# Norm offsets and relu moved to GpSimd, a causal mask in 64-row halves, and new instruction orders in the attention stage of an adaLN transformer block

## What is computed

```
mod = (silu(c) @ wmod) -> sa, ca, ga, sb, cb, gb          # one row of 256 each per sequence
h = layernorm(x) * (1 + ca) + sa
q, k, v = split(h @ w_qkv); rope(q), rope(k)               # 16 heads of 16
q, k = elu(q * scale) + 1, elu(k * scale) + 1              # the features
out_t = (q_t . sum_{s<=t} k_s v_s) / (q_t . sum_{s<=t} k_s)  # causal linear attention
x = x + ga * (out @ w_out)
h = layernorm(x) * (1 + cb) + sb
x = x + gb * moe(h)                                        # top 2 of 8 experts, gelu, 256 -> 1024 -> 256
```

## Time and profile before

| what | value |
|---|---|
| time, median of 3 runs | 820.7 us (819.55 to 820.79) |
| the profiled execution's own time | 825.53 us |
| its span | 823.2 us |
| busy: TensorE, VectorE, ScalarE, GpSimd | 737.3, 663.8, 580.3, 514.3 us |
| attention stage, about | 0 to 378 us |
| routing | 378 to 411 us |
| expert stage, about | 411 to 820 us |

### The profile page before, as it was taken

How to read it: one execution, slowest core, us unless ns; L and a number is a source line. 1 busy time by engine, 2 the same in 40 slices (tenths; PEclk the granted TensorE clock), 3 DMA queues, 4 the chain that set the end, 5 groups by cost and what they waited for, 6 DMA issues and landing times.

```text
span 823.2 us, 26404 instructions
## 1 busy us (share of the span) xinstructions
PE 737.3 (90%) x7949; PEld 540.3 (66%) x7949; DVE 663.8 (81%) x1488; ACT 580.3 (71%) x1103; POOL 514.3 (62%) x504
## 2 busy tenths in 40 slices
PE   6599999999999999973489999999999999999994
PEld 3366666666666666652367777777777777777772
DVE  2789999999999999965857777778777877777773
ACT  1478888888888888862057777777677767677762
POOL 3547576766666575744746666666676667667653
PEclk9799999999999999995589999999999999999998
DMA  6214333333333333310023333343334334343320
GB/s 207 86 41 126 107 115 111 107 108 105 111 113 114 109 116 115 112 53 32 21 79 75 73 71 69 68 78 70 73 73 76 66 69 78 66 76 70 74 31 0
DMA packets 52814, 68.78 MB, mean 84 GB/s; under 512 B 8864, under 2 KB 44080, under 8 KB 52736
## 3 DMA queue, kind: packets, MB, share of 16 engines
q0 software_dynamic: 18176, 27.06, 17.5%
q1 hardware_dynamic: 34560, 40.61, 16.0%
HBM read 46.50 MB, written 22.05 MB: 83 GB/s over the span
## 4 chain that ended last, share of the span: by engine, by line
PE 59%; DVE 16%; issue 10%; ACT 8%; POOL 3%; DMA 1%; DVEq 1%; another core or an unknown queue 0%; ACTq 0%; SPq 0%; POOLq 0%
PE hidden L1334 15%; PE bank L1350 15%; PE hidden L1336 8%; PE bank L1352 7%; PE bank L1189 5%; PE hidden L1172 3%; DVE amlo L511 2%; DVE nb L452 2%; PE bank L1172 2%; ACT feat L969 2%; ACT rb L968 2%; DVE rb L498 2%; DVE hT L475 2%; DVE st L432 2%; ACT qstT L932 1%
## 5 line engine op out<-in xcount | busy, mean ns | idle before, releaser
L1334 PE MATMUL hidden<-qstT,w1hi_k 128*128 128x256 f16 x1136 | 200.2, 274 | 1.1 <-DVE am L723 1.1
L1336 PE MATMUL hidden<-qstT,w1lo_k 128*128 128x128 f16 x1136 | 195.5, 220 | 0.0
L1350 PE MATMUL bank<-w,amhi 128*128 x568 | 188.6, 379 | 0.4
L1352 PE MATMUL bank<-w,amlo 128*128 x568 | 154.8, 273 | 0.0
L729 DVE TENSOR_TENSOR amlo<-am,amhi 128x512 f16<-128x512 f32 x142 | 98.4, 693 | 62.6 <-ACT am L1064 50.8
L919 POOL DMA_INDIRECT out_dram<-x,si x71 | 121.9, 1717 | 36.5 <-issue 27.4
L1334 PEld LDWEIGHTS hidden<-qstT,w1hi_k 128*128 x1136 | 111.7, 98 | 14.9 <-issue 1.3
L1336 PEld LDWEIGHTS hidden<-qstT,w1lo_k 128*128 x1136 | 111.7, 98 | 1.1
L1189 PE MATMUL bank<-wq,hT 128*128 128x256 f32 (+1 forms) x256 | 102.9, 528 | 9.2 <-DVE hT L475 9.1
L1063 ACT ACTIVATE amhi<-am 128x512 f16<-128x512 f32 x142 | 88.5, 623 | 12.6 <-DVE am L723 7.6
L1350 PEld LDWEIGHTS bank<-w,amhi 128*128 128x128 f16 x568 | 55.5, 98 | 62.3 <-issue 2.6
(11 more groups left out here) (203 smaller groups left out, 1814.2 us busy)
## 6 DMA issues: line engine op xcount, KB each, us to landing
stage<-in_L_ffn_w_dram SPq DMA_DIRECT2D x32, 512.0 KB, 4.1
xt<-in_L_attn_x_dram SPq DMA_DIRECT2D x32, 128.0 KB, 2.1
out_dram<-x SPq DMA_DIRECT2D x32, 128.0 KB, 1.7
ffn_rows<-h SPq DMA_DIRECT2D x32, 128.0 KB, 3.3
ffn_rows<-am SPq DMA_DIRECT2D x32, 128.0 KB, 3.1
am<-mod_rows SPq DMA_DIRECT2D x16, 128.0 KB, 3.6
mod_b<-mod_rows SPq DMA_DIRECT2D x8, 256.0 KB, 3.6
w<-in_L_wmod_dram SPq DMA_DIRECT2D x6, 256.0 KB, 4.4
```

The costliest lines, as they stand in the source:

```text
L1334: t.matmul(dst.rearrange("p (q n) -> p q n", q=2), w1s[0][k][g][:, w_], both, start=(k == 0), stop=False)
L1336: last = t.matmul(dst[:, P:2 * P], w1s[1][k][g][:, w_], both[:, 0, :], start=False, stop=(k == KT - 1))
L1350: t.matmul(y[:, :], ghi[:, m.p, c_m], w2s[mt // 2][:, bass.ds(w_, 2 * D)], start=(mt == 0), stop=False)
L1352: last = t.matmul(y[:, D:2 * D], glo[:, m.p, c_m], w2s[mt // 2][:, bass.ds(w_, D)], start=False, stop=(mt == MT - 1))
```

## The change

- The norm offset `nb` is no longer one VectorE instruction. VectorE writes minus the mean (`nm`, a 128x2 tensor_scalar, in an order slot after `ve`), and GpSimd multiplies it with rstd (`nb`, after `rs`).
- The relu of the features is no longer on ScalarE. GpSimd does it as a new step `rl` (128x512, f32, maximum with 0), and `f` waits for it too.
- The mask is added by four matmuls of 64 rows and 256 columns for a group in place of two of 128 rows and 512 columns. Key row 0 of a half is never masked by the triangle, so that it is used to mask all late keys for early queries. GpSimd fills 22 constants instead of 12 for this.
- All five orders are new.

```diff
-ORDER_PE = (("aT", 4), ("ear", 3), ("pj", 4), ("sc1", 3), ("hT", 0), ("pv0", 3), ("Tk", 2), ("h2T", 6), ("v", 0),
-            ("Tq", 2), ("lg", 6), ("pv1", 3), ("state", 2), ("sc0", 2), ("qk", 0))
-ORDER_DVE = (("f", 2), ("st", 0), ("st2", 5), ("mv", 0), ("mv2", 5), ("ve", 0), ("sl0", 3), ("nb", 0), ("rope", 1),
-             ("x1", 4), ("stl", 3), ("hTe", 0), ("sl1", 3), ("wlo", 1), ("den", 3), ("rec", 3), ("vlo", 0), ("at", 3))
-ORDER_POOL = (("shk", 2), ("rs", 0), ("slo", 2), ("R", 1), ("xm2", 5), ("h2", 5), ("wb", 2))
-ORDER_ACT = (("exp", 2), ("sh0", 3), ("shq", 2), ("sth", 3), ("aTe", 4), ("whi", 1), ("xn", 0), ("xn2", 5),
-             ("sh1", 3), ("kTs", 2), ("h2Te", 6), ("vhi", 0), ("qTs", 2), ("lge", 6))
-ORDER_SP = (("ldx", 0), ("ld", 1), ("ro", 6), ("modgb", 6), ("gb", 6), ("modg", 6), ("modb", 7), ("so", 4))
+ORDER_PE = (("aT", 4), ("ear", 3), ("sc1", 3), ("pv0", 3), ("pj", 4), ("Tk", 2), ("state", 2), ("h2T", 6), ("hT", 0),
+            ("pv1", 3), ("Tq", 2), ("v", 0), ("lg", 6), ("sc0", 2), ("qk", 0))
+ORDER_DVE = (("f", 2), ("st2", 5), ("sl0", 3), ("st", 0), ("mv2", 5), ("mv", 0), ("stl", 3), ("ve", 0), ("nm", 0),
+             ("rope", 1), ("sl1", 3), ("x1", 4), ("hTe", 0), ("den", 3), ("wlo", 1), ("rec", 3), ("vlo", 0),
+             ("at", 3))
+ORDER_POOL = (("shk", 2), ("slo", 2), ("rs", 0), ("nb", 0), ("R", 1), ("xm2", 5), ("wb", 2), ("rl", 1), ("h2", 5))
+ORDER_ACT = (("exp", 2), ("sh0", 3), ("shq", 2), ("sth", 3), ("whi", 1), ("aTe", 4), ("sh1", 3), ("xn", 0),
+             ("kTs", 2), ("xn2", 5), ("h2Te", 6), ("qTs", 2), ("vhi", 0), ("lge", 6))
+ORDER_SP = (("ldx", 0), ("ro", 6), ("modg", 6), ("modb", 7), ("so", 5), ("ld", 0), ("modgb", 6), ("gb", 6))
...
-            def offset(m):
-
-                wait(dve, a_["rs"], m.n + 1)
-                wait(dve, a_["xn"], m.n, NC)
-                wait(dve, a_["xn2"], m.n - NORM2)
-                v.scalar_tensor_tensor(out=nb[:, :], in0=mv[:, :, 0], scalar=-1.0, in1=rstd[:, :],
-                                       op0=ALU.mult, op1=ALU.mult).then_inc(a_["nb"], 1)
+            def negated(m):
+
+                wait(dve, a_["mv"], m.n + 1, NC)
+                wait(dve, a_["mv2"], m.n - NORM2 + 1)
+                wait(dve, a_["nb"], m.n)
+                v.tensor_scalar(neg_mean[:, :], mv[:, :, 0], -1.0, None, ALU.mult).then_inc(a_["nm"], 1)
...
             def features(m):
 
                 wait(dve, a_["exp"], m.n + 1)
+                wait(dve, a_["rl"], m.n + 1)
...
+            def offset(m):
+
+                wait(pool, a_["rs"], m.n + 1)
+                wait(pool, a_["nm"], m.n + 1)
+                carry(pool)
+                g.tensor_tensor(nb[:, :], neg_mean[:, :], rstd[:, :], ALU.mult).then_inc(a_["nb"], 1)
...
+            def positive(m):
+
+                wait(pool, a_["R"], m.n + 1)
+                carry(pool)
+                g.tensor_scalar(rb[:, :], ra[:, :], 0.0, None, ALU.max).then_inc(a_["rl"], 1)
...
-            def relu_exp(m):
+            def exponent(m):
                 wait(act, a_["R"], m.n + 1)
                 wait(act, a_["slo"], m.n)
-                v.activation(rb[:, :], ra[:, :], ACT.Relu)
                 v.activation(feat[:, :], ra[:, :], ACT.Exp).then_inc(a_["exp"], 1)
...
-                for odd in range(2):
-                    t.matmul(bank[5 + odd].rearrange("p (h t) -> p h t", t=P), ident_b[:, :],
-                             later[:, :].rearrange("p (u t) -> p u t", u=1).broadcast_to([P, 4, P]),
-                             start=True, stop=False, skip_group_check=True)
+                half = P // 2
+                for late_q in range(2):
+                    for odd in range(2):
+                        r = slice(odd * half, (odd + 1) * half)
+                        t.matmul(bank[5 + odd].rearrange("p (h t) -> p h t", t=P)[:, :, late_q * half:(late_q + 1) * half],
+                                 mask_row[r, late_q, :],
+                                 later[r, late_q, :].rearrange("p (u t) -> p u t", u=1).broadcast_to([half, 4, half]),
+                                 start=(late_q == 0), stop=False, skip_group_check=True)
```

More of the change, by code:

```diff
@@ L58 @@
 Q_SCALE = WS * float(HD ** -0.25)
-ORDER_PE = (("aT", 4), ("ear", 3), ("pj", 4), ("sc1", 3), ("hT", 0), ("pv0", 3), ("Tk", 2), ("h2T", 6), ("v", 0),
-            ("Tq", 2), ("lg", 6), ("pv1", 3), ("state", 2), ("sc0", 2), ("qk", 0))
-ORDER_DVE = (("f", 2), ("st", 0), ("st2", 5), ("mv", 0), ("mv2", 5), ("ve", 0), ("sl0", 3), ("nb", 0), ("rope", 1),
-             ("x1", 4), ("stl", 3), ("hTe", 0), ("sl1", 3), ("wlo", 1), ("den", 3), ("rec", 3), ("vlo", 0), ("at", 3))
-ORDER_POOL = (("shk", 2), ("rs", 0), ("slo", 2), ("R", 1), ("xm2", 5), ("h2", 5), ("wb", 2))
-ORDER_ACT = (("exp", 2), ("sh0", 3), ("shq", 2), ("sth", 3), ("aTe", 4), ("whi", 1), ("xn", 0), ("xn2", 5),
-             ("sh1", 3), ("kTs", 2), ("h2Te", 6), ("vhi", 0), ("qTs", 2), ("lge", 6))
-ORDER_SP = (("ldx", 0), ("ld", 1), ("ro", 6), ("modgb", 6), ("gb", 6), ("modg", 6), ("modb", 7), ("so", 4))
+ORDER_PE = (("aT", 4), ("ear", 3), ("sc1", 3), ("pv0", 3), ("pj", 4), ("Tk", 2), ("state", 2), ("h2T", 6), ("hT", 0),
[7 more added lines that the diff above has]
+ORDER_SP = (("ldx", 0), ("ro", 6), ("modg", 6), ("modb", 7), ("so", 5), ("ld", 0), ("modgb", 6), ("gb", 6))
 NORM2 = 5
-BOTH_NORMS = ("ve", "rs", "nb")
+BOTH_NORMS = ("ve", "nm", "rs", "nb")
 LAG_C = 2
@@ L136, in adaln_block @@
         ident16 = sb("ident16", [P, P], F16)
-        ident_b = sb("ident_b", [P, P], BF16)
-        later = sb("later", [P, P], BF16)
+        mask_row = sb("mask_row", [P, 2, P], BF16)
+        later = sb("later", [P, 2, P // 2], BF16)
         upto = sb("upto", [P, P], F16)
@@ L161, in adaln_block @@
         nb = sb("nb", [P, 2])
+        neg_mean = sb("neg_mean", [P, 2])
         h = sb("h", [P, D])
@@ L266, in counters @@
             return {k: sem(prefix + k) for k in names.split()}
-        a_ = counters("a_", "st mv ve rs nb xn hT hTe v vhi vlo qk rope R exp f shq shk slo Tq qTs Tk kTs"
+        a_ = counters("a_", "st mv ve nm rs nb xn hT hTe v vhi vlo qk rope R rl exp f shq shk slo Tq qTs Tk kTs"
                             " state sth stl ear sc0 sh0 sl0 sc1 sh1 sl1 pv0 pv1 den rec at aT aTe pj"
@@ L384, in carry @@
             eng.sem_inc(s_carry, 1)
-        POOL_CONST = 16
-        POOL_TWO, POOL_EROW = 37, 50
+        POOL_CONST = 26
+        POOL_TWO, POOL_EROW = 47, 60
         POOL_IDENT, POOL_FIRST = 2, 4
@@ L563, in _ @@
                 "st": first_stats, "mv": lambda m: mean_var(m, 0, "st", "mv"),
-                "ve": steadied, "nb": offset, "hTe": h_modulated, "vlo": v_low,
+                "ve": steadied, "nm": negated, "hTe": h_modulated, "vlo": v_low,
                 "rope": rope, "f": features, "sl0": lambda m: scores_low(m, 0), "sl1": lambda m: scores_low(m, 1),
@@ L753, in attention_constants @@
                 link(g.memset(ident16[:, :], 0.0))
-                link(g.memset(ident_b[:, :], 0.0))
-                link(g.memset(later[:, :], 0.0))
+                link(g.memset(mask_row[:, :, :], 0.0))
+                link(g.memset(later[:, :, :], 0.0))
                 link(g.memset(v16[:, :, 0, :, HD:VW], 1.0))
@@ L758, in attention_constants @@
                 link(g.memset(state[:, :, :, :], 0.0))
[L759 to L763, removed]
+                diagonal(ident16)
+                link(g.affine_select(out=upto[:, :], in_=upto[:, :], compare_op=ALU.is_ge, fill=0.0, base=0,
+                                     pattern=[[1, P]], channel_multiplier=-1))
+                half = P // 2
+                for u in range(2):
+                    r = slice(u * half, (u + 1) * half)
+                    for late_q in range(2):
+                        link(g.affine_select(out=mask_row[r, late_q, :], in_=mask_row[r, late_q, :],
+                                             compare_op=ALU.not_equal, fill=1.0, base=-half * late_q,
+                                             pattern=[[1, P]], channel_multiplier=-1))
+                    link(g.affine_select(out=later[r, :, :], in_=later[r, :, :], compare_op=ALU.is_ge, fill=MASKED,
+                                         base=0, pattern=[[0, 2], [1, half]], channel_multiplier=-1))
+                    link(g.memset(mask_row[u * half:u * half + 1, 0, 0:half], 0.0))
+                    link(g.memset(mask_row[u * half:u * half + 1, 0, half:P], 1.0))
+                    link(g.memset(later[u * half:u * half + 1, 0, :], MASKED))
                 assert link.n == POOL_CONST, link.n
@@ L785, in root @@
                 wait(pool, a_["ve"], m.n + 1)
-                wait(pool, a_["nb"], m.n)
                 wait(pool, a_["xn"], m.n, NC)
@@ L836, in rotated @@
                 g.tensor_tensor(ra[:, :], ra[:, :], rb[:, :], ALU.add).then_inc(a_["R"], 1)
+            def positive(m):
+                wait(pool, a_["R"], m.n + 1)
+                carry(pool)
```

(7 more changed lines are left out.)

## The result

| what | before | after |
|---|---|---|
| time, median | 820.7 us | 854.4 us (852.74 to 855.23, 4 runs) |
| ratio to before, 95% interval | | 1.0402 [1.0377, 1.0427] |
| the profiled execution's own time, its span | 825.53, 823.2 us | 854.35, 852.6 us |

The change makes the kernel 4.0% slower. The forecast was slower too, but by 7 us; measured are 33.7 by the medians, and 854 lies above the range of 800 to 842. The profiled execution of before was 4.8 above its median and that of after is at its median, so the two traces differ by 28.8 only.

What follows compares the result with a forecast made beforehand. VectorE was taken to bound the attention stage, 10.50 us an iteration; 30 x (10.35 - 10.50) = -4.5, 7 x 1.6 = +11.2, start +1 and drain -1 made +6.7, so 832 profiled and 828 as median; range 800 to 842.

Steps and rivals of the forecast that it cites:

- as walked: VectorE and GpSimd: `xm2` runs between the halves of `wlo`, which run 7.1 to 7.7 and 8.4 to 9.0.
- the 0.32 and 0.18 taken: GpSimd: `nb` taken to run 0.32, near a 128x32 product, with 0.18 ahead of it waiting for `rs`.
- I take 0.7, near the cast: GpSimd: duration taken for `rl`, near the 0.61 cast of 128x512, the only one-input row of that length.
- from above 1.27: GpSimd: upper bound for `rl`, from the two-input sum of 128x512.
- my own walk: Attention stage: one new iteration laid out from the start of `f`, 10.35 ordinarily and 11.95 with `wb`.
- `ve` "unblocked": VectorE: only instructions with two SBUF inputs were said to exclude GpSimd's; `ve` and `nm` end at 3.6, after `stl` at 3.4.
- TensorE and its clock: TensorE: full clock, 3 us idle in 40, not the bound; mask saving of 0 to 0.6 an iteration counted as nothing.
- `wb` at 1.6: GpSimd: `wb` between `xm2` and `rl` once in four iterations, 1.6 more each, seven times, +11.2.
- Rival B: GpSimd: `rl` takes 1.27 and ends at 10.2, `h2` at 10.9; +23, 844; chance 0.10.
- C: Rival at `f`: it takes its turn ahead of `h2`; ordinary iteration 9.95, with `wb` 11.3; -7, 814; chance 0.22.
- D: Rival: no collisions, `xm2` and `wlo` don't meet; iteration about 9.6, with `wb` 10.5; -21, 800; chance 0.20.

## Why the direction was right and the size wrong

**Right, as the runs show.** `f` waits for `rl` (14.7 in after, 16 times) and then for its turn behind `h2` (1139 ns, and 692 with `h2` ahead of `rl`); `xm2` meets `wlo`, whose pair takes 1.81 as walked; the offset is late and `xn` waits for it; an iteration with `wb` is longer; the shorter mask changes nothing (1.0020, and 0.9922 against 0.9905 with the norm steps); `nb` on GpSimd, 0.20 with 0.20 ahead of it, is 0.1 under the 0.32 and 0.18 taken.

**The term that failed: "I take 0.7, near the cast"** for `rl`. It takes 1.49 where nothing stretches it, as in most iterations with `wb` in after. Even "from above 1.27", my upper bound, was too low: a two-input sum was no bound for a one-input instruction of another form. The warning stood in the earlier trace rows, where a tensor_scalar of 72 columns takes 0.39; I named it and chose the cast all the same. The Trainium skill's price by "GPSIMD Engine Reference", Performance versus the Vector engine, 769 ns, is half of what this form takes; the copy's 607 lies below it. With 1.49 in my own walk the ordinary iteration is 10.35 + 0.8, and one with `wb` 12.75: 30 x 0.65 + 7 x 1.6 = +31, which is the measured 30.8. That it agrees so closely is partly luck, since other terms were off against each other:

- **`ve` "unblocked"** was wrong. A tensor_scalar of two columns stands still beside `slo` (203.65 to 204.29, where `slo` ends at 204.26), and `rs` begins at 204.45. The Trainium skill has it in "SBUF — State Buffer", Who interferes with whom, where a tensor_scalar on VectorE is among those that can, under conditions, meet GpSimd; I had taken two-input instructions alone. For `rs` it costs only 0.1, as `slo` had to end first; for VectorE and so for `wlo` it costs 0.47.
- **TensorE and its clock** were put at nothing, though its order is new: the walk has no row for it. In the iteration shown `Tk` takes 0.45 more at the lower clock and `hTe` waits 0.43 for `hT`; that and `ve` make the 0.8 by which `xm2` ends later than walked. The wait for `hT` comes in 7 of 22 iterations, and the clock between 100 and 340 us is 0.95. With `rl` early it is 1.00 in the same new TensorE order. What the clock costs over all iterations no run isolates.
- **`wb` at 1.6** was too much. Between 100 and 360 us of after, iterations with it take 12.3 to 12.9 and the others 11.3 in the mean, so about 1.2; `rl` behind it is mostly not stretched. Moving it away gave back 5 us in all.

**Rival B** (the late `rl`, 0.10) was the right mechanism with too small a price, 844 at 1.27. C needed `rl` and D `xm2` done earlier than they were.

**What the walk did not show** is that the losses come by a combination. In after `xm2` is late, and `rl` behind `xm2` hands this on to `f`:

| norm steps on GpSimd | `rl` | orders of the other engines | ratio |
|---|---|---|---|
| before `slo` | behind `R` | old | 0.992 |
| before `slo` | behind `xm2`, `wb` | old | 1.000 |
| behind `slo` | behind `R` | new | 1.000 |
| behind `slo` | behind `xm2`, `wb` | new | 1.040 |

From the first row to the last it is 4.8%, of which `rl`'s place is 0.75% with the old orders and 4% with the new. The new rows differ from the old in the orders of VectorE, TensorE, ScalarE and SP too. So it is shown that the place of `rl` costs so much only together with the new orders; that `nb` behind `slo` is what makes them so is argued from the two traces (`xm2` at 7.5 and at 6.0 behind `f`). The one run that moves the norm steps ahead of `slo` with TensorE's, ScalarE's and SP's new orders, `rl` behind `R` and `wb` last, has 1.022, worse than the third row. What each engine's new order costs by itself stays open: with TensorE's old list and the others new, the one try gave 1.17.

## What to carry to other kernels

Price a moved instruction by its own form on its new engine, not by the nearest length: 128x512 took 0.61 as a cast, 1.27 as a sum and 1.49 as a maximum with a constant. Put the new step where that engine idles and ahead of steps that wait for others; the same 1.5 us cost 4% behind a waiting step and nothing ahead of it. Try the edits in the old orders first: here they gain 0.8% there (0.95% with the norm steps alone), and the new orders turn that into 4% of loss. A stretched instruction is worth freeing only if nothing else is awaited in its time (`wlo`, mask and norm steps alone: about 0.65 us an iteration freed where its instructions went from 1.02 to 0.68, and 1.9 of waiting for `pv1` found).

## What the runs showed of the hardware

- On GpSimd a tensor_scalar with maximum, 128x512 f32 to f32, took 1.49 us; a copy of the same tile 0.61 in its fastest instance, but about 1.07 in the median beside VectorE's work.
- A one-input VectorE instruction of 2 columns (`ve`) took up to 1192 ns in after, beside a two-input GpSimd instruction, and 170 in the mean without one.
- The one-input `rl` and the two-input `wlo` ran side by side unstretched when `rl` had begun 0.68 to 0.82 earlier, in the run with `rl` behind `R`. `rl` took 1.93 when it began during a half of `wlo`, in after. With all edits in the old orders, where `rl` had begun 0.1 to 0.2 earlier, it took 1.49 in most iterations and the pair of `wlo` about 1.6. I have not found the rule for this pair.
- Four matmuls of 64 rows and 256 columns, which use the two halves of the rows, took 0.39 for the group against 0.59 for two of 128 rows and 512 columns.
- Eight transposes of 128x128 (`Tk`) took 1.06 in a stretch of 0.57 of the clock and 0.61 at the full clock, in after.
